# Perceiver kernel: the sweep's running sums for each head in two column tiles instead of for each pair of heads

## What is computed

```python
q_prime = relu(einsum('bhnd,fd->bhnf', q, Wqf))
k_prime = relu(einsum('bhnd,fd->bhnf', k, Wkf))      # 16 heads, 6272 rows, 64 features
k_prime = k_prime * attention_mask[:, None, :, None]
kv      = einsum('bhnf,bhne->bhfe', k_prime, v)      # for each head 64 x 16, summed over 6272 rows
k_sum   = sum(k_prime, axis=2)                       # for each head 64 numbers
out     = einsum('bhmf,bhfe->bhme', q_prime, kv) / (einsum('bhmf,bhf->bhm', q_prime, k_sum)[..., None] + 1e-08)
```

## Time and profile before

| | |
|---|---|
| median of 3 runs | 1456.51 us (1454.06 to 1457.14) |
| profiled execution, its own time | 1455.31 us |
| span from its first to its last instruction | 1453.2 us |
| mean granted TensorE clock over the span | 0.928 of 2.4 GHz |
| TensorE streams (PE) busy | 1298.1 us, 89% |
| TensorE loads (PEld) busy | 790.2 us, 54% |
| VectorE busy | 902.6 us, 62% |
| ScalarE busy | 675.8 us, 47% |
| GpSimd busy | 20.2 us, 1% |

### The profile page before, as it was taken

The page is one execution under the profiler, slowest core; times in us unless marked ns, Lnnn a source line. Parts: engine busy times, 40 slices in busy tenths (PEclk is TensorE's granted clock), DMA queues, the critical chain, the costliest instruction groups (busy, mean ns, idle before and its releaser), DMA issues.

```text
span 1453.2 us, 19202 instructions
## 1 busy us (share of the span) xinstructions
PE 1298.1 (89%) x5968; PEld 790.2 (54%) x5968; DVE 902.6 (62%) x2123; ACT 675.8 (47%) x1412; POOL 20.2 (1%) x41
## 2 busy tenths in 40 slices
PE   8999999997679996879889999999999999668968
PEld 5666666665334443525346565665656568333533
DVE  3556555558668885426968778787878773432244
ACT  2222222221137774123768778787878774010201
POOL 0000000001000000000000000000000000000000
PEclk9999999996789996788999999999999999777969
DMA  5000000001200003751000000000000002222013
GB/s 214 25 14 29 14 14 29 14 4 69 77 26 2 0 1 154 318 205 55 0 0 1 1 1 0 0 0 0 0 0 0 0 1 82 80 86 81 1 49 124
DMA packets 11794, 64.43 MB, mean 44 GB/s; under 512 B 1376, under 2 KB 2016, under 8 KB 8160
## 3 DMA queue, kind: packets, MB, share of 16 engines
q1 hardware_dynamic: 11312, 63.08, 12.0%
q10 hardware_dynamic: 432, 0.72, 0.1%
HBM read 63.72 MB, written 0.07 MB: 44 GB/s over the span
## 4 chain that ended last, share of the span: by engine, by line
PE 76%; ACT 10%; DVE 8%; issue 4%; DMA 1%; POOL 1%; SPq 0%; DVEq 0%; ACTq 0%; POOLq 0%; PEldq 0%
PE ps L2017 10%; PE ps L1983 9%; PE ps L1394 9%; PE ps L1358 7%; PE ps L1676 6%; PE ps L2003 4%; PE ps L1404 4%; PE ps L1381 3%; ACT wide L2374 2%; ACT wide L2377 2%; PE ps L2509 2%; PE ps L2011 2%; PE ps L2488 2%; DVE x_keys L2206 2%; PE ps L1944 1%
## 5 line engine op out<-in xcount | busy, mean ns | idle before, releaser
L1983 PE MATMUL ps<-keysT,row_biases_sb 128*128 128x512 f32 (+1 forms) x416 | 189.2, 579 | 0.0
L2017 PE MATMUL ps<-vals,x_probsT 128*128 128x256 f32 x784 | 186.0, 379 | 0.3 <-ACT x_probsT L2394 0.3
L2017 PEld LDWEIGHTS ps<-vals,x_probsT 128*128 128x128 f32 x784 | 147.3, 190 | 53.6 <-issue 37.5
L1394 PE MATMUL ps<-ring,S 128*128 128x512 f32 (+1 forms) x392 | 134.6, 486 | 1.0 <-DVEq L1460 1.0
L1445 ACT ACTIVATE S<-ps 128x512 f32<-128x512 f32 x98 | 53.2, 595 | 154.6 <-PE ps L1404 154.6
L1676 PE MATMUL ps<-keysT,vals 128*128 (+2 forms) x208 | 108.3, 611 | 5.4 <-DVE vals L1749 2.7
L1983 PEld LDWEIGHTS ps<-keysT,row_biases_sb 128*128 128x128 f32 x416 | 77.6, 193 | 63.7 <-issue 48.8
L1358 PEld LDWEIGHTS ps<-S 128*128 128x128 f32 x816 | 96.6, 194 | 18.5 <-DVE S L1483 16.2
L2003 PE MATMUL ps<-x_keys,x_q 128*128 128x512 f32 (+1 forms) x208 | 102.8, 576 | 1.9 <-DVE S L2217 1.9
L1358 PE MATMUL ps<-S 128*128 128x33 f32 x816 | 102.2, 281 | 2.3 <-POOL sw_key_out L1538 2.3
L1481 DVE TENSOR_SCALAR S<-ps,mask_sb 128x256 f32<-128x256 f32 x49 | 23.7, 483 | 128.5 <-PE ps L1394 128.5
(11 more groups left out here) (425 smaller groups left out, 2024.3 us busy)
## 6 DMA issues: line engine op xcount, KB each, us to landing
ring<-weights SPq DMA_DIRECT2D x24, 1024.0 KB, 4.9
ring<-weights SPq DMA_DIRECT2D x8, 864.0 KB, 4.4
keysT<-ctxT SPq DMA_DIRECT2D x1, 6272.0 KB, 18.9
vals<-ctxN SPq DMA_DIRECT2D x1, 6272.0 KB, 21.2
S<-ctxT SPq DMA_DIRECT2D x12, 512.0 KB, 3.9
ring<-weights SPq DMA_DIRECT2D x6, 768.0 KB, 5.6
row_biases_sb<-row_biases SPq DMA_DIRECT2D x1, 1416.0 KB, 12.3
ring<-weights SPq DMA_DIRECT2D x1, 1008.0 KB, 8.8
```

Of the source, the lines that this page charges most:

```text
L1394: ins = pe.matmul(ps[0:TILE, b, 0:m], sw_ctxT[ph][:, k, TILE * s:TILE * s + TILE], w[:, 512 + 768 * k + a:512 + 768 * k + a + m], start=k ...
L1983: ins = pe.matmul(ps[:, c % 3, 0:width(c)], x2_wk[:, k, :], ctxT[:, k, span(c)], start=k == 0, stop=k == KT - 1)
L2017: ins = pe.matmul(bank(6, D), x2_probsT[:, c % 2, 128 * s:128 * s + 128], ctxN[:, SUB * c + s, :], start=c == 0 and s == 0, stop=c == NC - ...
```

## The change

`add_sums` no longer makes one product for a pair of heads but one for each head: the stationary operand is the 64 feature columns of one head, the moving operand its own 16 values and the mask, 17 columns. The products of even heads are written to partitions 0 to 63 of PSUM, those of odd heads to partitions 64 to 127, so they lie in two different column tiles of the array, 64 columns wide each, and one head of each comes in turn. `sw_values` gets 16 blocks of 17 columns in place of 8 of 33 (272 columns for 264), so the buffers behind it move by a few columns, and the mask column is written 16 times for each row rather than 8 times. The last copies read the blocks where they now lie.

```diff
-        sw_values = [cut(scratch(5120 + 264 * i, 264, TILE), PAIRS, 33) for i in range(2)]
+        sw_values = [cut(scratch(5120 + 272 * i, 272, TILE), NH, 17) for i in range(2)]
...
-                for j in range(PAIRS):
-                    ins = pe.matmul(sums[:, 33 * j:33 * j + 33], sw_features[buf][:, 128 * j:128 * j + 128], sw_values[buf][:, j, :],
+                for h in range(NH):
+                    half = slice(FD * (h % 2), FD * (h % 2) + FD)
+                    ins = pe.matmul(sums[half, 17 * (h // 2):17 * (h // 2) + 17], sw_features[buf][:, FD * h:FD * h + FD], sw_values[buf][:, h, :],
                                     start=start, stop=stop, skip_group_check=True)
...
-                    dve.tensor_scalar(sw_values[s % 2][:, :, 0:32], cut(ps[0:TILE, 2, 0:D], PAIRS, 32), m, None, ALU.mult)\
+                    dve.tensor_scalar(sw_values[s % 2][:, :, 0:HD], cut(ps[0:TILE, 2, 0:D], NH, HD), m, None, ALU.mult)\
                        .then_inc(sem("sw_part"), 1)
-                    dve.tensor_copy(sw_values[s % 2][:, :, 32:33], m.unsqueeze(1).broadcast_to([TILE, PAIRS, 1]))\
+                    dve.tensor_copy(sw_values[s % 2][:, :, HD:HD + 1], m.unsqueeze(1).broadcast_to([TILE, NH, 1]))\
                        .then_inc(sem("sw_values_ready"), 1)
...
-            total = cut(ps[:, 6, 0:33 * PAIRS], PAIRS, 33)
+            total = cut(ps[:, 6, 0:17 * PAIRS], PAIRS, 17)
             for e in range(2):
                 half = slice(T * e, T * e + T)
-                dve.tensor_copy(sweep_sums[half, :, HD * e:HD * e + HD], total[half, :, HD * e:HD * e + HD]).then_inc(sem("sw_sums"), 1)
-                dve.tensor_copy(sweep_sums[half, :, 32 + e:33 + e], total[half, :, 32:33]).then_inc(sem("sw_sums"), 1)
+                dve.tensor_copy(sweep_sums[half, :, HD * e:HD * e + HD], total[half, :, 0:HD]).then_inc(sem("sw_sums"), 1)
+                dve.tensor_copy(sweep_sums[half, :, 32 + e:33 + e], total[half, :, HD:HD + 1]).then_inc(sem("sw_sums"), 1)
```

More of the change, by code:

```diff
@@ L1324, in perceiver @@
         sw_features = [scratch(3072 + 1024 * i, 1024, TILE) for i in range(2)]
-        sw_values = [cut(scratch(5120 + 264 * i, 264, TILE), PAIRS, 33) for i in range(2)]
-        sw_key = scratch(5648, D, TILE)
-        sw_absmax, sw_step, sw_inv = scratch(5904, 16, TILE), scratch(5920, 16, TILE), scratch(5936, 16, TILE)
+        sw_values = [cut(scratch(5120 + 272 * i, 272, TILE), NH, 17) for i in range(2)]
+        sw_key = scratch(5664, D, TILE)
+        sw_absmax, sw_step, sw_inv = scratch(5920, 16, TILE), scratch(5936, 16, TILE), scratch(5952, 16, TILE)
         sw_key_both = sb("sw_key_out", [TILE, 2, D])
         sw_key_out = [sw_key_both[:, i, :] for i in range(2)]
-        sw_value_absmax = scratch(5952, D)
+        sw_value_absmax = scratch(5968, D)
         sw_value_part = sb("sw_value_part", [128, D])
-        value_inv = scratch(5952, D, TILE)
+        value_inv = scratch(5968, D, TILE)
         value_tmp = wide[:, :, :].rearrange("p a n -> p (a n)")
```

## The result

The kernel takes **1421.74 us** (median of 4 runs, 1418.83 to 1423.61) where the kernel before takes 1456.73 (median of 4, 1454.06 to 1457.14): a ratio of 0.9762, 95% interval 0.9741 to 0.9782, so 2.4% faster. The forecast was 1424 us. The profiled execution took 1418.83 us, its span is 1416.8 us (before 1453.2), and the mean granted clock is 0.928 as before.

The account below looks back on a forecast made before the run. TensorE alone was taken to bound the sweep, with loads setting the pace in the sums. 1455.31 - 33 (50 calls at 0.66 us) + 0.5 for the last call = 1422.8; the median stands 1.2 higher, so 1424 us; 8-in-10 range 1414 to 1473.

Parts of the forecast that it names:

- TensorE sets the pace, and the sums' loads within it: In the sweep TensorE alone bounds, 5.80 us a tile; in the sums loads take the time, 0.111 us each before.
- A load of 64 columns is 0.058 us, as in the earlier trace: In the sums, a load 128 rows by 64 columns follows the last at 0.058 us, half of 0.111.
- Column tiles load side by side: In the sums, both column tiles load at once, 16 pairs each at 0.058 us; 1424 us, chance 0.57.
- rival one: In the sums, column tiles don't overlap: 16 more steps, 0.93 us, 13.5 us slower in all, 1470 us; chance 0.26.
- rival two: In the sums, a head's two passes hold each other up: 24 steps for 16, 10 us saved, 1446 us; chance 0.12.
- rival three: In the sums, upper-half loads cost the whole width's 0.111 us: 56 us over the kernel before, 1512 us; chance 0.03.
- rival four: In the sweep, TensorE's clock lost for a tenth of it gives back 30 us, time about as before; chance 0.02.
- The new change of shape: Between sums and transposes, the transposes' load starts 0.07 us before the streams' end instead of 0.27, at 1.04 us.
- 0.66 us saved in a call: From the sums' first load to the transposes' first, 1.04 us in place of 1.70; 50 calls, 33 us.
- the idle time that the prediction named as a sign: Ahead of the transposes' first load, an idle time absent before the change would appear; no size given.
- Nothing becomes late, VectorE's edits are hidden: In a tile, VectorE and ScalarE still wait 2 us, no buffer becomes the bound, and VectorE's edits count as nothing.
- All behind the sweep as before: Everything behind 339 us stays as before, only earlier, but for a few us from the clock's changes.

## Why the prediction was right, point by point

- **TensorE sets the pace, and the sums' loads within it.** Right. The tile is the chain's PE throughout, and longer streams change nothing (1421.28 with 33 columns, 1421.74 with 17).
- **A load of 64 columns is 0.058 us, as in the earlier trace rows.** Right: 0.058 in one tile, and in two tiles the 32 loads take what 16 steps take.
- **Column tiles load side by side.** Right, and it carried the sign, as the prediction said: 1421.74 against 1469.19 for the same loads in one tile, where rival one had 1470. Of the two pages of the Trainium skill that stood against each other there, "TensorEngine Tiling (Array Packing)", Key Properties (different tiles load and multiply in parallel) agrees with these runs. "TensorE: Matmul & The Clock Gate", Part 3, The mechanism (loads overlap with matmuls in flight only when the row group differs) doesn't: both column tiles use all 128 rows.
- **The two passes of a head don't hold each other up (rival two).** Right that they don't, and the runs say why it isn't close: not every load has to alternate, three may stand in between.
- **Upper half as dear as the whole width (rival three), a lower clock (rival four).** Neither. 32 loads in 1.01 us leave no room for a dearer half. The granted clock is 1.00 through the sweep, and the loads' pace of 0.058 us is that of the earlier trace rows. The pace is the better witness: for the stretch from 2 to 6 us of the kernel before the windows print 1.00 as well, and there the same 16 loads, the first after 2.25 us in which TensorE stood idle, took 3.49 us for 1.86, so the granted clock by itself doesn't show that TensorE works at 2.4 GHz.

```profile
2.00:6.00 4.00, 3.62 (x16) 3.49 (x16) 0.00 (x0) 1.28 (x1) 0.72 (x3) 1.00 0.97 332
```

- **The new change of shape.** It is there: the transposes' load at 0.07 us before the stream's end, as forecast, at 1.05 us (forecast 1.04). The run with two more changes of shape has a price of 0.15 us each, without a new wait for another engine. The prediction charged 0.20, and kept 1414 for none.
- **0.66 us saved in a call.** It was 0.74 in a tile, and this is the term that was mis-sized, by 0.08 x 49 = 3.9 us: the profiled execution took 1418.83 where the sum had 1422.8, and the sweep ended at 301.89 + 0.44 = 302.3 where it was to end near 306. The prediction measured to the first load of the transposes, and took what comes behind it as unchanged. But in the earlier trace rows that load starts earlier than the pace has it: the last load of the sums ended at 203.86 + 1.86 = 205.72, so with its 0.19 began at 205.53, and the transposes' began 0.03 us later, where 0.111 is the pace. The load is the longer, 184 ns in the median where it is 140 after the change, and the projections' load came 205.81 - 205.56 = 0.25 behind. After the change it begins only when the last load of the sums has ended (194.69 for 193.64 + 1.01 = 194.65, the idle time that the prediction named as a sign, of 0.04 us), and the projections' load follows at 194.86 - 194.69 = 0.17. Measured from the sums' first load to the projections' first load, before had 205.81 - 203.86 = 1.95 and after has 1.22: 0.73. The end point of a difference has to be an instruction whose own surroundings don't change. The last call saved 0.4 us where the prediction took 0.66 - 0.5 = 0.16, since its wait for VectorE's last key was 0.15 us; against that stands the later start of the first tile's sums, 0.45 us, which no part of the change explains.
- **Nothing becomes late, VectorE's edits are hidden.** Right: VectorE's wait fell by what the tile lost (0.73 us for 0.74), TensorE's streams wait for another engine once between 11 us and the sweep's end, 0.9 us in the first tile, as before (1.0), and VectorE is busy for the same 3.21 us in a tile.
- **All behind the sweep as before.** Right to 0.1 us: span and sweep are both 36.4 us shorter.

The median fell by 35.0 us and not by 36.4: the profiled execution after the change was the fastest of four, 2.9 us under their median, while the one before lay 1.4 under its own.

## What to carry to other kernels

Where loads of the stationary operand set the pace and the streams are short, split the operand into column tiles, and let them come in turn: two tiles of 64 nearly halved the time of the sums and four of 32 made it about a third (1.90, 1.04, 0.67 us), though the number of matmuls doubled each time. With four, look at the places where a hardware loop begins anew. Put the tiles' matmuls next to each other in the queue, no more than four loads of one tile in a row, and keep groups of one shape together, for each change of shape cost about 0.15 us here. And measure a saving up to an instruction on whose own neighbours nothing changes.

## What the runs showed of the hardware that wasn't expected

- Loads of another column tile are started past waiting ones, but not past many: by the rule that fits these orders, at most three (1.01 us for turns of two loads, 1.03 for four, 1.32 for eight, 1.73 for sixteen).
- With four column tiles 64 loads and 64 streams of 17 columns go in 0.67 us, but TensorE then loses 0.33 to 0.51 us wherever the hardware loop starts a new round; with two column tiles it loses nothing there. A pair of a load and a stream then comes each 0.67 / 64 = 0.010 us, while a load by itself lasts 0.109.
- The loads of the transposes, also 128 columns wide, follow each other at 0.20 - 0.14 = 0.06 us where the others of that width are at 0.111. Why, no run here asked.
- The first keys of the sweep wait for a DMA that landed between 6.87 us (before) and 9.47 us (four tiles) over these nine profiles, without any order in it. By the first tile's sums it is 17.39 to 19.30 us: up to 1.9 us of a difference between two profiles of this kernel are that. The cause is open.
